# A four-layer graph network on one Trainium2 core: first weights and support of the last layer as half-precision pairs

## What is computed

```python
x = layernorm(x + prelu(adj @ (x @ W) + bias))          # L0
x = layernorm(x + (adj @ (x @ weight) + bias))          # L1
x = layernorm(x + gated(x, adj != 0, 5 rounds of GRU))  # L2
x = layernorm(x + groups(x, adj))                       # L3
```

```python
h     = relu(norm_adj @ (x_g @ W1[g]) + b1[g])
out_g = relu(norm_adj @ (h @ W2[g]) + b2[g])
fused[:, idx, :] += softmax(fusion_w)[g] * out_g
```

## Time and profile before

| | us |
|---|---|
| median of 3 runs (lowest, highest) | 990.35 (988.59, 992.75) |
| the profiled execution | 988.7 |
| its span, first to last instruction | 986.9 |
| TensorE busy in the span | 950.6 |
| VectorE, ScalarE, GpSimd busy | 820.8, 770.9, 749.0 |

### The profile page before, as it was taken

How to read it: one execution, slowest core, us unless ns; L and a number is a source line. 1 busy time by engine, 2 the same in 40 slices (tenths; PEclk the granted TensorE clock), 3 DMA queues, 4 the chain that set the end, 5 groups by cost and what they waited for, 6 DMA issues and landing times.

```text
span 986.9 us, 19418 instructions
## 1 busy us (share of the span) xinstructions
PE 950.6 (96%) x6010; PEld 574.5 (58%) x6010; DVE 820.8 (83%) x2077; ACT 770.9 (78%) x1324; POOL 749.0 (76%) x844
## 2 busy tenths in 40 slices
PE   7999998999999999999999999999999999989894
PEld 6999996554444544444554555554445455468783
DVE  5999998898879999988898899789879987946555
ACT  5698896888887877887887889788887977865552
POOL 4777888567989897987988798889778887974101
PEclk9999999999999999999999999999999999999997
DMA  7543450333744563375448345654943563440020
GB/s 191 132 119 108 131 129 18 63 72 65 118 75 65 102 115 81 59 133 105 81 80 154 76 66 115 115 107 89 164 88 55 108 127 67 77 91 18 26 66 28
DMA packets 295406, 90.74 MB, mean 92 GB/s; under 512 B 222514, under 2 KB 295175, under 8 KB 295303
## 3 DMA queue, kind: packets, MB, share of 16 engines
q1 hardware_dynamic: 295302, 89.49, 45.8%
HBM read 28.67 MB, written 8.81 MB: 38 GB/s over the span
## 4 chain that ended last, share of the span: by engine, by line
PE 71%; DVE 10%; POOL 6%; issue 6%; ACT 3%; DMA 2%; SPq 0%; POOLq 0%; DVEq 0%; ACTq 0%
PE psum L1560 16%; PE psum L1565 16%; PE psum L1561 16%; PE psum L1485 8%; PE psum L1592 6%; POOL shared L765 2%; PE psum L1640 2%; PE psum L1673 2%; DMA shared<-shared 1%; DVE x3q L1020 1%; PE psum L1659 1%; PE psum L1483 1%; DVE shared L1342 1%; PE psum L1518 1%; DVE shared L1349 1%
## 5 line engine op out<-in xcount | busy, mean ns | idle before, releaser
L765 POOL TENSOR_TENSOR shared<-shared 128x512 f32<-128x512 f32 x160 | 203.7, 1273 | 34.6 <-ACT shared L974 34.5
L724 POOL TENSOR_TENSOR shared<-shared 128x512 f16<-128x512 f32 x128 | 148.3, 1158 | 52.9 <-ACT shared L928 52.8
L1565 PE MATMUL psum<-shared,wx_hi 128*128 128x512 f16 x480 | 182.1, 379 | 2.0 <-DVE shared L1368 1.7
L1560 PE MATMUL psum<-shared,wh_hi 128*128 128x512 f16 x480 | 182.2, 380 | 0.5 <-DVE shared L1342 0.4
L1560 PE MATMUL psum<-shared,wx_hi 128*128 128x512 f16 x480 | 181.9, 379 | 0.0
L1561 PE MATMUL psum<-shared,wx_lo 128*128 128x512 f16 x480 | 181.9, 379 | 0.0
L1565 PE MATMUL psum<-shared,wh_hi 128*128 128x512 f16 x480 | 181.9, 379 | 0.0
L1561 PE MATMUL psum<-shared,wh_lo 128*128 128x512 f16 x480 | 181.9, 379 | 0.0
L1342 DVE SCALAR_TENSOR_TENSOR shared<-psum,bhn,shared 128x512 f32<-128x512 f32 x160 | 119.9, 749 | 52.4 <-ACT shared L945 49.9
L974 ACT ACTIVATE shared<-psum,brz,unscale 128x512 f32<-128x512 f32 x160 | 124.2, 776 | 46.2 <-PE psum L1565 46.1
L910 ACT ACTIVATE shared<-psum 128x512 f16<-128x512 f32 x160 | 95.6, 597 | 52.7 <-PE psum L1592 52.7
(11 more groups left out here) (183 smaller groups left out, 1742.8 us busy)
## 6 DMA issues: line engine op xcount, KB each, us to landing
m<-in_adj_dram SPq DMA_DIRECT2D x32, 256.0 KB, 3.0
m<-in_x_dram SPq DMA_DIRECT2D x32, 256.0 KB, 3.4
adjr<-in_adj_dram SPq DMA_DIRECT2D x32, 256.0 KB, 3.2
out_dram<-x SPq DMA_DIRECT2D x8, 768.0 KB
shared<-shared SPq DMA_TRANSPOSE x192, 3.2
out_dram<-shared SPq DMA_DIRECT2D x32, 50.0 KB
v<-in_L_gnn_W_dram SPq DMA_DIRECT2D x10, 128.0 KB, 2.4
x3q<-x SPq DMA_DIRECT2D x16, 50.0 KB
```

Source lines behind the costliest of these rows:

```text
L724: nc.gpsimd.tensor_tensor(HT_LO[s % 2], HT[s][:, :], HT_HI[s % 2], ALU.subtract).then_inc(b_htl, 1)
L765: nc.gpsimd.tensor_tensor(ZH[s % 2][:, :], ZW[s % 2][:, :], HT[s][:, :], ALU.mult).then_inc(b_zh, 1)
L1560: mm(dst, w_h[:, col:col + P], h[:, :], start=start, stop=False)
L1565: return mm(dst, w_h[:, col:col + P], lo[:, :], start=False, stop=stop)
```

## The change

**The first weights and the support become pairs of half-precision tiles.** W1 is scaled by a number for each group (`ups`), cut into W1_HI and W1_LO, and the support into SP_HI and SP_LO with one scale. `hid` does three passes (W1_HI by SP_HI, W1_LO by SP_HI, W1_HI by SP_LO) in place of one float32 product. b1 is scaled to match (`b1_over`), and the copies to TT take the scale out (`unscale_c`). `support_out` writes SP_HI, and VectorE's new `support_rest` writes SP_LO; the third pass of the first half waits for it.

**The scales are found on the chip**, in `second_scales`, one or two operations in a slot of the middle stage: absolute values on ScalarE and their largest on VectorE, of anT (slots 71 to 74 and 83 to 86) and of W1 (90 to 94 and 103 to 107), a transpose and a product on TensorE (110 and 116), small operations on VectorE (112, 113 and 123 to 126), W1_HI on ScalarE (130 to 134), W1_LO on VectorE (143 to 147). v1's loads are issued in slots 71 to 75, v2's in 128 to 132.

**Order and buffers.** The first support copy is issued at the start of slot 162, ahead of the last tanh. HID lies over RT and ZW; the first relus wait for the last state (`b_h`), and the copies to TT wait for `b_fl`. The steps are written with a count for each (`IN_STEP`), which is 16 for all eight.

```diff
-        SP_T = part([P, CS])
+        SP_HI, SP_LO = part([P, CS], F16), part([P, CS], F16)
...
-        HID = [part([P, CS]) for c in range(HC)]
...
+        assert used[0] <= RT_AT
+        used[0] = RT_AT
+        HID = [part([P, CS]) for c in range(HC)]
...
+            def second_scales(t):
+                if t in AN_ABS_AT:
+                    i = AN_ABS_AT.index(t)
+                    act.wait_ge(l3_v, L3_AN)
+                    lo, hi = AN_CUT[i], AN_CUT[i + 1]
+                    nc.scalar.activation(cmp_a[:, lo:hi], anT[:, lo:hi], ACT.Abs).then_inc(v_abs, 1)
+                if t in W1_ABS_AT:
+                    i = W1_ABS_AT.index(t)
+                    act.wait_ge(w_ld_v1, 16 * NG)
+                    act.wait_ge(v_top, 4)
+                    nc.scalar.activation(v2[:, i * W1:(i + 1) * W1], w1_in[i], ACT.Abs).then_inc(v_abs, 1)
+                if t in W1_HI_AT:
+                    i = W1_HI_AT.index(t)
+                    act.wait_ge(v_scale, V_SCALED)
+                    act.wait_ge(an_st, 16)
+                    act.wait_ge(a_z1, STEPS_A)
+                    nc.scalar.activation(W1_HI[i], w1_in[i], ACT.Identity, scale=ups[:, i:i + 1]).then_inc(v_hi, 1)
...
             def support_out(k):
                 act.wait_ge(c_s, k + 1)
-                nc.scalar.activation(SP_T[:, :].rearrange("p (b x) -> p b x", b=2),
-                                     psum[:, 2 * 512:4 * 512].rearrange("p (b x) -> p b x", b=2)[:, :, 0:CS // 2],
-                                     ACT.Copy).then_inc(c_st, 1)
+                if k == 0:
+                    act.wait_ge(v_scale, V_SCALED)
+                b = by_bank(IN_STEP[k])
+                nc.scalar.activation(SP_HI[:, :].rearrange("p (b x) -> p b x", b=2)[:, 0:b, :],
+                                     psum[:, 2 * 512:4 * 512].rearrange("p (b x) -> p b x", b=2)[:, 0:b, 0:CS // 2],
+                                     ACT.Identity, scale=ups[:, NG:NG + 1]).then_inc(c_st, 1)

             def slot_b(at, t):
+                if t == ITEMS + 2:
+                    support_out(0)
...
+            def second_scales(t):
+                def step(ins, signal, value):
+                    ins.then_inc(signal, 1)
+                    dve.wait_ge(signal, value)
+                if t in AN_TOP_AT:
+                    i = AN_TOP_AT.index(t)
+                    dve.wait_ge(v_abs, i + 1)
+                    nc.vector.tensor_reduce(an_tops[:, i:i + 1], cmp_a[:, AN_CUT[i]:AN_CUT[i + 1]], AX_X, ALU.max)\
+                      .then_inc(v_top, 1)
+                if t in W1_TOP_AT:
+                    i = W1_TOP_AT.index(t)
+                    dve.wait_ge(v_abs, 4 + i + 1)
+                    nc.vector.tensor_reduce(tops[:, i:i + 1], v2[:, i * W1:(i + 1) * W1], AX_X, ALU.max)\
+                      .then_inc(v_top, 1)
+                if t == W1_TOP_AT[-1] + 1:
+                    dve.wait_ge(v_top, 4)
+                    nc.vector.tensor_reduce(tops[:, NG:NG + 1], an_tops[:, :], AX_X, ALU.max).then_inc(v_top, 1)
+                if t == TURN_AT + 2:
+                    dve.wait_ge(v_turn, 1)
+                    nc.vector.tensor_reduce(top_of[:, :], bank[5][0:NG + 1, 0:P], AX_X, ALU.max).then_inc(v_top, 1)
+                if t == TURN_AT + 3:
+                    dve.wait_ge(v_top, V_TOPS + 1)
+                    nc.vector.tensor_scalar(top_diag[:, :], ident[0:NG + 1, 0:NG + 1], top_of[:, 0:1], None, ALU.mult)\
+                      .then_inc(v_top, 1)
+                if t == SCALE_AT:
+                    dve.wait_ge(v_turn, 2)
+                    step(nc.vector.tensor_scalar(tops[:, :], bank[5][:, 0:NG + 1], 1e-15, None, ALU.max), v_scale, 1)
+                    step(nc.vector.reciprocal(ups[:, :], tops[:, :]), v_scale, 2)
+                if t == SCALE_AT + 1:
+                    step(nc.vector.tensor_scalar(ups[:, :], ups[:, :], W_LIMIT, None, ALU.mult), v_scale, 3)
+                    step(nc.vector.tensor_scalar(ups[:, NG:NG + 1], ups[:, NG:NG + 1], 1.0 / (NODES * X_TOP), None,
+                                                 ALU.mult), v_scale, 4)
+                if t == SCALE_AT + 2:
+                    step(nc.vector.tensor_scalar(over[:, :], ups[:, 0:NG], ups[:, NG:NG + 1], None, ALU.mult),
+                         v_scale, 5)
+                    step(nc.vector.reciprocal(unscale_c[:, :], over[:, :]), v_scale, 6)
+                if t == SCALE_AT + 3:
+                    nc.vector.tensor_tensor(b1_over.rearrange("p (g c) -> p g c", c=HC),
+                                            b1T.rearrange("p (g c) -> p g c", c=HC),
+                                            over[:, :].unsqueeze(2).to_broadcast([P, NG, HC]), ALU.mult)\
+                      .then_inc(v_scale, 1)
+                if t in W1_LO_AT:
+                    i = W1_LO_AT.index(t)
+                    dve.wait_ge(v_hi, i + 1)
+                    if i >= 3:
+                        dve.wait_ge(v_lo, 3)
+                        dve.wait_ge(v_hi, 2)
+                    nc.vector.scalar_tensor_tensor(W1_LO[i], w1_in[i], ups[:, i:i + 1], W1_HI[i],
+                                                   ALU.mult, ALU.subtract).then_inc(v_lo, 1)
+
+            def support_rest(k):
+                b = by_bank(IN_STEP[k])
+                dve.wait_ge(c_st, k + 1)
+                if k == 0:
+                    dve.wait_ge(v_scale, V_SCALED)
+                nc.vector.scalar_tensor_tensor(
+                    SP_LO[:, :].rearrange("p (b x) -> p b x", b=2)[:, 0:b, :],
+                    psum[:, 2 * 512:4 * 512].rearrange("p (b x) -> p b x", b=2)[:, 0:b, 0:CS // 2],
+                    ups[:, NG:NG + 1], SP_HI[:, :].rearrange("p (b x) -> p b x", b=2)[:, 0:b, :],
+                    ALU.mult, ALU.subtract).then_inc(c_sl, 1)
...
+                if has(0) and k > 0:
+                    support_rest(k)
                 if has(3):
                     apply_q(k - 3)
...
+            def second_scales(t):
+                if t == TURN_AT:
+                    pe.wait_ge(v_top, V_TOPS)
+                    nc.tensor.transpose(bank[5][0:NG + 1, 0:P], tops[:, :], ident[:, :]).then_inc(v_turn, 1)
+                if t == TURN_AT + 6:
+                    pe.wait_ge(v_top, V_TOPS + 2)
+                    mm(bank[5][:, 0:NG + 1], ones_rows[:, :], top_diag[:, :], start=True, stop=True)\
+                        .then_inc(v_turn, 1)
...
                 def hid(c, lo):
-                    for g in range(NG):
-                        last = mm(by_group(lo, g), v1[:, (g * HC + c) * P:(g * HC + c + 1) * P],
-                                  slots(SP_T[:, :], g), start=True, stop=True)
+                    passes = ((W1_HI, SP_HI), (W1_LO, SP_HI), (W1_HI, SP_LO))
+                    for i, (w, t) in enumerate(passes):
+                        if i == 2 and c == 0:
+                            pe.wait_ge(c_sl, k + 1)
+                        for g in range(NG):
+                            last = mm(by_group(lo, g, IN_STEP[k]), w[g][:, c * P:(c + 1) * P],
+                                      slots(t[:, :], g, IN_STEP[k]), start=i == 0 and g < 2,
+                                      stop=i == 2 and g >= NG - 2, skip_group_check=True)
                     last.then_inc(c_h[c], 1)
...
-V_LOAD = 108
+V1_LOAD, V2_LOAD = 71, 128
+AN_ABS_AT, AN_TOP_AT = (71, 72, 73, 74), (83, 84, 85, 86)
+W1_ABS_AT, W1_TOP_AT = (90, 91, 92, 93, 94), (103, 104, 105, 106, 107)
+TURN_AT, SCALE_AT = 110, 123
+W1_HI_AT, W1_LO_AT = (130, 131, 132, 133, 134), (143, 144, 145, 146, 147)
+V_TOPS, V_SCALED = 10, 7
+X_TOP = 11.4
```

180 lines of the change are left out of this document (110 added, 70 removed).

## The result

The changed kernel has a median of 993.63 us (8 runs, 992.75 to 995.28), the kernel before 990.24 on the same chip (8 runs, 988.29 to 992.75). The ratio is 1.0037, with a 95% interval of 1.0022 to 1.0053: some 3.4 us are lost; the interval reaches just past the 0.5% band, so at that band the loss can't be called. The profiled execution took 992.75 us with a span of 991.0, against 988.7 and 986.9 before.

The account below looks back on a forecast made before the run. The middle stage was taken as bound by TensorE, the last stage by a chain over engines. Middle stage +4.8 us and last stage -1.4 us gave +3.4 on 990.35, some 993.7 us; range 987.5 to 999.

Parts of the forecast that it names:

- ScalarE's 14 operations: Middle stage: absolute values and scaled copies ahead of the R sigmoid, one a slot, cost 0.15 us each, 2.1 us.
- VectorE, held operations and small chains: Middle stage: eight SBUF-only operations that may find GpSimd busy cost 0.27 us each, 2.2 us, plus 0.1 for small chains.
- TensorE's transpose and product: Middle stage: a transpose of 128 float32 columns and a tiny product, each between others, add 0.4 us.
- transfers, and what is left: Middle stage: the moved V1 and V2 loads cost nothing, or 1 us if they are late.
- start of the last stage: Copy ahead of the last tanh, relu no longer waiting for GpSimd: second weights start earlier, 0.5 us gained.
- six ordinary steps: Last stage: half-precision passes shorten the first product, 0.47 us gained in each step, 2.8 us in all.
- fourth step: Last stage: VectorE's new operation delays the queued statistics, powers, normalisations and relus, adding 1.8 us.
- end: After the last step nothing covers the scaled copies into TT, so they cost 0.1 us.
- above 1 us each: Sign in the profile after: the W1_LO operations on VectorE in slots 143 to 147 last over 1 us each.
- The row that spoke against it, L1376: VectorE operation of W1_LO's form, 0.68 us without wait; by it the five would be hidden and the term 0.8 us.
- The third pass's wait: Sign in the last stage: a gap of 0.3 us before the third pass of the first half, which needs SP_LO.
- the 1.6 us of low clock: Fourth step: the time lost to low clock in the second weights stays as it was, between 0.8 and 2.5 us.

Follow-up runs that it names:

- e1_places: Changed kernel with VectorE's middle-stage work ahead of L1453 (q), not L1466, and ScalarE's behind the R sigmoid: 991.48 us, 1.0018 to the kernel before.
- e2_q_behind: Changed kernel with VectorE's L1508 behind the work left from the middle stage in each last-stage step: 993.17 us, 1.0036 to the kernel before.
- e3_start_back: Changed kernel with ScalarE's support copy back behind the last tanh and VectorE's rest behind the last state: 994.48 us, 1.0050 to the kernel before.

## Why the prediction came out right, term by term

| term | predicted us | profile after, us |
|---|---|---|
| ScalarE's 14 operations | 2.1 | 0.97 |
| VectorE, held operations and small chains | 2.3 | 2.25 |
| TensorE's transpose and product | 0.4 | 0.58 |
| transfers, and what is left | 0 | -0.15 |
| start of the last stage | -0.5 | +0.13 |
| six ordinary steps | -2.8 | -1.70 |
| fourth step | +1.8 | +1.87 |
| end | +0.1 | +0.10 |
| sum | +3.4 | +4.1 |

The second column is worked out from differences of slot spacings and of the starts of the support product, in one profile of each kernel; the fourth line is what is left of 3.65, and the last step counts as the sixth ordinary one up to its second weights. The spans differ by 991.0 - 986.9 = 4.1 us and the medians by 3.4.

**Right.** VectorE's operations: W1_LO 0.33 each and the three held small ones, in slots 124 to 126, 0.19, where 0.27 was taken for all eight. The sign "above 1 us each" held for four of the five W1_LO; the first took 0.90. That they wait for GpSimd is shown by their ends beside L754's and by e1_places. The Trainium skill, page "SBUF — State Buffer", section "Who interferes with whom", says so of two SBUF inputs, and of some one-input forms; the five-column scaling is of the latter, and the reductions, which it exempts, took 0.36 us for 207 columns, as their row has it, with a spread of 0.003. At these places the trace agrees with the page:

```profile
L1360 DVE TENSOR_REDUCE scales_c<-v x4: 358/360/361, 525.5 to 538.0; 128x1 f32<-128x207 f32 x3, 128x1 f32<-128x206 f32 x1
```

The row that spoke against it, L1376, had stood where nothing on GpSimd read SBUF; at 169.52 us of the trace before, where L765 was running, the same L1376 took 1.25 us instead of 0.68. Place, and not form, decided, as the prediction took it. The fourth step: 13.08 us to the second weights where 12.8 was forecast, and e2_q_behind confirms the queue as the cause. The third pass's wait was 0.25 where 0.3 was said.

**Right by luck in part: the clock in the fourth step.** The prediction kept the 1.6 us of low clock, with bounds of 0.8 and 2.5. In the changed kernel's profile they were 4.89 - 3.41 = 1.5. In e1_places and e3_start_back, which have the same code in this step and start the second weights after the same 13.07 us, they were 3.0 and 2.7 (6.41 and 6.11 us), beyond the bound, and the step took 19.31 and 19.02 us. So +1.87 is what this one profile has; with their clock it would be +3.4 and +3.1.

**Mis-sized: ScalarE's term.** "0.15 each" holds for the five W1_HI (0.14), which last 0.49 us like L806. The shorter ones cost 0.05 and nothing, and the spacing forecast for slots 90 to 94, 4.45 to 4.5, came out at 4.38. The step that failed is "the new ones have more columns, so I take 0.15": the nine absolute values are shorter than L806 (0.36 and 0.40 us), and a length is paid only beyond the slack of its place. That slack can be read in the traces. In an undisturbed slot TensorE starts the next item's product in R's bank 0.31 us after the sigmoid's end (570.10 and 570.41 before), in every slot with one of ScalarE's added operations 0.14 us after it (742.83 and 742.97, with a W1_HI): 0.17 of slack. Another 0.07 is ScalarE's idle time earlier in the slot. Records that follow each other overlap by 0.10, so operations of 0.36, 0.40 and 0.49 put the sigmoid back by 0.26, 0.30 and 0.40, against a slack of some 0.25. ScalarE's idle time just ahead of L945, "next to nothing", did not show it; what a known length costs did, 0.49 for 0.13 in the earlier trace rows.

**Mis-sized: the ordinary step.** 11.3, not 11.1, and the gain 0.29, not 0.47. The step that failed is the pace of a pass, 0.44 ns a column, taken from products of 128 columns; the products of 400, 144 and 112 columns took 0.47 to 0.58 ns a column. A pass takes (957.12 - 956.23) / 2 = 0.44 us and not 0.40, so three take 1.32: in the individual records the products of 400, 144 and 112 columns follow each other at 0.19, 0.08 and 0.07 where I had counted 0.17, 0.06 and 0.056. In the first half the pass behind the wait made it 1.59 instead of 1.55. These two halves explain it: 0.29 and 0.10 saved, 0.09 lost in ScalarE's copy.

**Only as the clock has it.** The start gains 0.55 us as forecast where the clock stays at 2.4 GHz, and nothing in the profile of the changed kernel, where it fell, a case that the prediction had only in its bound. The total was hit by luck: a middle stage smaller by 1.1 us than forecast (3.65 for 4.8) and a last stage worse by 1.8 (+0.4 for -1.4) largely cancel.

**Not forecast: 0.9 us less in slots 120 and 121.** 0.7 of them are VectorE's. In all three float32 profiles VectorE's mask of an adjacency tile (L1323) there had to wait for its load, started beside GpSimd's L735 and took 1.2 to 1.4 us; in the changed kernel the load landed about 1 us earlier, and the same operation, L1446, took 0.42:

```profile
691.72 1.33 DVE L1323 TENSOR_SCALAR shared<-adjr 128x512 f16<-128x512 f32 x1 [0.17 <-DMA adjr<-in_adj_dram]
```

What stays open is why that load lands earlier. The loads of v1 and v2, no longer issued from slot 108 to 117, are the nearest difference; no run moves them by themselves. The other 0.2, and the few slots that wait 0.1 to 0.4 more, differ from profile to profile of the same code.

## What to carry to other kernels

An operation slipped into the queue of an engine that works beside a saturated TensorE costs its length less the slack at that very place; move it by one neighbour and measure again before it is made smaller. Where VectorE and GpSimd both work on SBUF, put the short VectorE operation where GpSimd waits for something, or ahead of one that has slack. And a chain of small operations over three engines is spread over several steps, not moved within one: a single constant gave some 4 us here, more than the whole change costs, and most of what looks like the gain of a new format belongs to the kernel before as well (ratio 0.9936 with the orders alone, 0.9920 and 0.9930 with both).
